# Projection and feed-forward output computed token-major, gates read as rows from a DRAM scratch

## What is computed

```
mod = cond @ ada_w.T + ada_b              # per sequence: six rows of 128
sh_msa, sc_msa, g_msa, sh_mlp, sc_mlp, g_mlp = split(mod, 6)
h  = modulate(rmsnorm(x), sh_msa, sc_msa)
q, k, v = split(h @ qkv_w.T)              # 16 heads of 8; rmsnorm and rope on q, k
o  = softmax(q k^T) v
x  = x + g_msa * (o @ proj_w.T + proj_b)  # x1 in the kernel
h2 = modulate(rmsnorm(x), sh_mlp, sc_mlp)
ff = (silu(h2 @ w1.T) * (h2 @ w3.T)) @ w2.T
x  = x + g_mlp * ff                       # x2 in the kernel
... second block: layer norm, q/k/v, linear attention, layer norm, silu, out_W, gate
```

## Time and profile before

| | |
|---|---|
| time, median of 3 runs | 212.8 us (212.53 to 213.04) |
| profiled execution, its own time | 211.97 us |
| its span, first to last instruction | 210.2 us |
| PE busy in the span | 183.4 us, 87% |
| DVE, POOL, ACT busy | 164.0, 135.9, 130.7 us |
| granted TensorE clock, mean | 0.987 of 2.4 GHz |

### The profile page before, as it was taken

The page is one execution under the profiler, slowest core; times in us unless marked ns, Lnnn a source line. Parts: engine busy times, 40 slices in busy tenths (PEclk is TensorE's granted clock), DMA queues, the critical chain, the costliest instruction groups (busy, mean ns, idle before and its releaser), DMA issues.

```text
span 210.2 us, 5867 instructions
## 1 busy us (share of the span) xinstructions
PE 183.4 (87%) x1986; PEld 141.1 (67%) x1986; DVE 164.0 (78%) x488; ACT 130.7 (62%) x354; POOL 135.9 (65%) x346
## 2 busy tenths in 40 slices
PE   1796868889999999899999999999998799998742
PEld 1544556667777777777776787788886478887522
DVE  4798898897979799996666434778899589999851
ACT  1476696677777777676555784453432367999740
POOL 8889798989786867758800783167512546757642
PEclk9999999999999999999999999999999999999995
DMA  5963000000000000000000000000000000001102
GB/s 111 280 178 142 0 5 3 0 0 3 3 3 2 3 6 0 3 3 2 3 3 0 3 3 0 2 0 0 6 0 0 0 2 3 0 25 30 51 26 74
DMA packets 9915, 5.13 MB, mean 24 GB/s; under 512 B 3025, under 2 KB 9758, under 8 KB 9758
## 3 DMA queue, kind: packets, MB, share of 16 engines
q1 hardware_dynamic: 6494, 4.08, 6.4%
q10 hardware_dynamic: 3392, 0.68, 1.6%
HBM read 3.71 MB, written 1.05 MB: 23 GB/s over the span
## 4 chain that ended last, share of the span: by engine, by line
PE 61%; DVE 21%; ACT 6%; issue 6%; POOL 2%; ACTq 2%; POOLq 0%; DVEq 0%
PE bank L1769 8%; DVE qkpad L1500 8%; PE bank L1778 7%; PE bank L1860 6%; PE bank L799 5%; PE bank L810 5%; PE bank L800 5%; PE bank L786 4%; PE bank L920 3%; PE bank L1801 2%; PE bank L1837 2%; PE bank L1872 2%; PE bank L852 2%; ACT probs L1201 2%; PE bank L1830 2%
## 5 line engine op out<-in xcount | busy, mean ns | idle before, releaser
L1201 ACT ACTIVATE probs<-bank 128x512 f32<-128x512 f32 x64 | 34.7, 594 | 22.6 <-PE bank L1778 22.5
L1500 DVE TENSOR_REDUCE qkpad<-bank 128x4 f32<-128x512 f32 x64 | 41.0, 684 | 9.1 <-PE bank L1769 7.7
L1778 PE MATMUL bank<-qTm,kBD 32*128 32x128 f32 x512 | 37.1, 283 | 0.4 <-ACT probs L1201 0.4
L1769 PE MATMUL bank<-kBD,qTs 32*128 32x256 f32 x224 | 31.7, 399 | 5.7 <-DVE qkpad L1500 4.2
L1778 PEld LDWEIGHTS bank<-qTm,kBD 32*128 32x128 f32 x512 | 31.0, 186 | 1.0 <-ACT probs L1201 0.6
L1769 PEld LDWEIGHTS bank<-kBD,qTs 32*128 32x128 f32 x224 | 19.8, 184 | 10.8 <-DVE qkpad L1500 7.4
L545 ACT ACTIVATE th<-bank 128x256 f32<-128x256 f32 x24 | 9.2, 384 | 18.9 <-PE bank L800 15.5
L1860 PE MATMUL bank<-probs,vpad 128*32 128x128 f32 x512 | 18.5, 277 | 0.2
L1051 POOL TENSOR_TENSOR partner<-qk,rope 128x96 f32<-128x96 f32 x32 | 14.3, 467 | 6.7 <-ACT qk L1243 6.7
L1801 PE MATMUL bank<-ident,qkpad 128*128 128x128 f32 x96 | 16.5, 281 | 0.8 <-DVE qkpad L1598 0.8
L481 POOL TENSOR_SCALAR var<-mv 128x2 f32<-128x2 f32 x16 | 3.1, 193 | 20.3 <-DVE mv L672 18.4
(11 more groups left out here) (250 smaller groups left out, 512.3 us busy)
## 6 DMA issues: line engine op xcount, KB each, us to landing
gate<-in_cond_dram SPq DMA_DIRECT2D x1, 1024.0 KB, 4.6
out_dram<-res SPq DMA_DIRECT2D x8, 128.0 KB, 1.8
xin<-in_x_dram ACTq DMA_DIRECT2D x2, 256.0 KB, 5.1
xin<-in_x_dram SPq DMA_DIRECT2D x1, 512.0 KB, 4.9
ada_n<-in_L_cond_ada_w_dram SPq DMA_DIRECT2D x1, 256.0 KB, 5.2
w_n<-in_L_cond_w_dram SPq DMA_DIRECT2D x2, 128.0 KB
qkv_n<-in_L_cond_qkv_w_dram SPq DMA_DIRECT2D x1, 192.0 KB, 3.9
w_n<-in_L_cond_w_dram SPq DMA_DIRECT2D x1, 170.5 KB
```

The source lines that it names most:

```text
L1201: q.activation(probs[2 * r + i][:, :, :, :].rearrange("p f a t -> p (f a t)"), bank[E_BANK[i]][:, :], ACT.Exp, scale=SCALE).then_inc(s_p, 1)
L1500: q.tensor_reduce(out_, score_bank(b, r, i)[:, :].rearrange("p (f a t) -> p f a t", f=2, a=2), X_AXIS, ALU.max, negate=True).then_inc(s_ma ...
L1769: last = q.matmul(bank[S_BANK[i]][:, f * 2 * T:(f + 1) * 2 * T], qTs[b % 2][rows, f, :], kBD[b % NKB][rows, f, :, :].rearrange("p a t -> p ...
L1778: last = q.matmul(bank[E_BANK[i]][:, (2 * f + k) * T:(2 * f + k + 1) * T], kBD[t % NKB][rows, f, k, :], qTm[t % 2][rows, f, :], start=True ...
```

## The change

The gates of the attention projection (`modr[:, 2]`), of its bias (`gbias`) and of the feed-forward (`modr[:, 5]`) are turned into rows on PE, copied by ACT, written to a DRAM scratch and read back by three DMAs that spread each over all partitions (`g1_rows`, `bias1_rows`, `g2_rows`, 1 MB each, in buffers that are free then: x2, y, res). POOL multiplies `projT` with the gate row of each sequence (`scaled_projection`) and adds the bias row to the input (`input_biased`). The projection has `oT` stationary and the scaled matrix moving, its result is token-major, and DVE adds the input straight from it. `projected` on ACT and `projected_turned` on PE are gone, batch statistics on DVE are replaced by a square with a sum on ACT, and `rms1` shrinks from seven operations to two. In the feed-forward `back` has ff stationary and w2T moving, two matmuls of 128 columns into banks 2 and 3 in place of one of 256; DVE multiplies both with the gate rows into `fg`, and POOL adds x1 (DVE for units 6 and 7). The transposes of fg are gone. `std2` of units 5 to 7 moves one place back on POOL's queue.

```
@@ blocks_gpsimd
+                cols = pair(u)
+                g.wait_ge(s_sq1, UNIT * u + UNIT)
+                q.tensor_scalar(ms1[:, cols], ms1[:, cols], 1.0, EPS0, ALU.mult, ALU.add).then_inc(b_ms, 1)
+                g.wait_ge(b_ms, u + 1)
                 q.tensor_tensor(rstd1[:, cols], ms1[:, cols], minus_half[:, 0:UNIT], ALU.pow).then_inc(b_rstd, 1)
...
+            def after_feed_forward(u):
...
+                g.wait_ge(b_fg, u + 1)
+                if u == 0:
+                    g.wait_ge(s_pg, B)
+                q.tensor_tensor(x2[:, pair(u), :], fg[u % 2][:, :, :], x1[:, pair(u), :], ALU.add).then_inc(b_x2, 1)
...
+            for u in range(start, U):
+                if u + 2 < U:
+                    rms1(u + 2)
+                normed1(u)
+                after_feed_forward(u - 3)
+                std2(u - 5)
+            after_feed_forward(U - 3)
+            std2(U - 5)
             std2(U - 4)
-            std2(U - 3)
...
+                if 1 <= t <= 3:
+                    std2(U - 4 + t)
@@ blocks_vector
-            def b_fed(t):
-                if is_unit(t):
-                    v.wait_ge(b_fm, t + 1)
...
+            def spread2(u):
+
+                v.wait_ge(b_x2, u + 1)
...
             def b_rest(t):
                 gated_(t, 0)
...
                 gated_(t, 1)
                 gate_(t, 2)
                 if is_unit(t):
-                    v.wait_ge(b_fgT, t + 1)
...
+                    v.wait_ge(b_fm, t + 1)
+                    if t == 0:
+                        v.wait_ge(ld_g2, 16)
+                    wait(v, b_x2, t - 1)
+                    for j in range(UNIT):
+                        last = q.tensor_tensor(fg[t % 2][:, j, :], bank[F_BANK[j]][:, 0:D], g2_rows[:, UNIT * t + j, :], ALU.mult)
+                    last.then_inc(b_fg, 1)
+                    if t >= JOINED:
...
+                        q.tensor_tensor(x2[:, pair(t), :], fg[t % 2][:, :, :], x1[:, pair(t), :], ALU.add).then_inc(b_x2, 1)
                 gated_(t, 2)
...
+                for u in ((t,) if t >= JOINED + 1 else (t - 1, t) if t == JOINED else (t - 1,)):
+                    if is_unit(u):
+                        spread2(u)
@@ blocks_tensor
-                    last = q.matmul(bank[F_BANK][:, 0:UNIT * T], w2T[:, c, :], ff[c][:, :], start=c == 0, stop=c == FC - 1)
+                    for j in range(UNIT):
+                        last = q.matmul(bank[F_BANK[j]][:, 0:D], ff[c][:, j * T:(j + 1) * T], w2T[:, c, :],
+                                        start=c == 0, stop=c == FC - 1)
...
-                if is_unit(t):
-                    e.wait_ge(b_fg, t + 1)
-                    wait(e, b_x2, t)
-                    turned(bank[FT_BANK], lambda j: fg[:, j, :], b_fgT)
@@ sync
+            sp.wait_ge(pv_a, A_ROWS)
+            sp.dma_start(scratch.rearrange("c b f -> b c f"), rows[:, :, :]).then_inc(ld_rows, 16)
+            sp.wait_ge(ld_rows, 16)
+            sp.dma_start(g1_rows[:, :, :], scratch[0, :, :].partition_broadcast(128)).then_inc(ld_g1, 16)
+            sp.dma_start(bias1_rows[:, :, :], scratch[1, :, :].partition_broadcast(128)).then_inc(ld_gb1, 16)
+            sp.wait_ge(pv_a, A_SQUARES)
+            sp.dma_start(g2_rows[:, :, :], scratch[2, :, :].partition_broadcast(128)).then_inc(ld_g2, 16)
@@ gpsimd
+            def scaled_projection(b):
...
+                g.wait_ge(ld_g1, 16)
+                g.wait_ge(pv_a, A_DONE)
+                wait(g, s_proj, b - 1)
+                q.tensor_tensor(projTg[b % 2][:, :], projT[:, :], g1_rows[:, b, :], ALU.mult).then_inc(s_pg, 1)
+
+            def input_biased(b):
...
+                g.wait_ge(ld_gb1, 16)
+                g.wait_ge(pv_a, A_SQUARES)
+                g.wait_ge(s_xs, b + 1)
+                q.tensor_tensor(xin[:, b, :], xin[:, b, :], bias1_rows[:, b, :], ALU.add).then_inc(s_xb, 1)
...
                 turned_own(t + 5)
-            blocks_gpsimd(g)
+                scaled_projection(t - 1)
+                input_biased(t - 1)
...
@@ scalar
-            def projected(b):
...
+            def spread_of(b):
...
+                a.wait_ge(s_x1, b + 1)
+                wait(a, s_sq1, b)
+                q.activation(squared[:, :], x1[:, b, :], ACT.Square, scale=D ** -0.5, accum_out=ms1[:, b:b + 1]).then_inc(s_sq1, 1)
...
+            q.activation(rows[:, :, :].rearrange("b c f -> b (c f)"), bank[O_BANK][0:B, 0:3 * D], ACT.Copy).then_inc(pv_a, 1)
             square_sums_of_rows()
@@ vector
-                v.wait_ge(s_prT, b + 1)
-                q.tensor_tensor(x1[:, b, :], bank[P_BANK][:, 256:384], xin[:, b, :], ALU.add).then_inc(s_x1, 1)
...
+                v.wait_ge(s_proj, b + 1)
+                v.wait_ge(s_xb, b + 1)
+                q.tensor_tensor(x1[:, b, :], bank[P_BANK][:, 384:512], xin[:, b, :], ALU.add).then_inc(s_x1, 1)
@@ tensor
                 e.wait_ge(s_oT, b + 1)
-                q.matmul(bank[P_BANK][:, 384:512], projT[:, :], oT[:, :], start=True, stop=True).then_inc(s_proj, 1)
+                e.wait_ge(s_pg, b + 1)
+                wait(e, s_x1, b)
+                q.matmul(bank[P_BANK][:, 384:512], oT[:, :], projTg[b % 2][:, :], start=True, stop=True).then_inc(s_proj, 1)
```

160 lines of the change are left out of this document (78 added, 82 removed).

## The result

| | before | after |
|---|---|---|
| time, median | 212.92 us (212.53 to 213.21, 4 runs) | 222.84 us (221.55 to 223.11, 4 runs) |
| profiled execution | 211.97 us | 222.69 us |
| its span | 210.2 us | 221.0 us |
| PE busy in the span | 183.4 us | 184.3 us |

The change makes the kernel slower by 4.6%: the ratio of the times is 1.0459, with a 95% interval from 1.0432 to 1.0485. The forecast was 220.9, with a range from 217.3 to 225.0. Of the 10.8 us that the span grew by, only 0.9 is busy time of PE (the net of matmuls that are gone and of stretches in which they run at half the clock), and 9.9 is PE waiting. An execution more than 1.5% above the fastest of its kernel is left out of the comparisons; there is one, in e7.

A forecast was written before the change was run, and what follows sets the result against it. PE bounds the feed-forward; a chain from DVE's row maxima through PE sets attention's 6.07 us step. Terms +2.7 - 0.3 + 0.3 + 6.3 - 0.9 = +8.1 on 211.97 give 220.1, plus 0.8 for the median 220.9; range 217.3 to 225.0.

The forecast's parts named there:

- step 3: Attention: PE's projection waits for POOL's scaled matrix, so round 1 starts at 52.95 instead of 50.86, +2.1 us.
- clock behind step 3: Attention, PE's clock after the long projection wait: no loss was forecast.
- steps 5 to 12: Attention: the loop through qk, Newton steps, POOL's product and projection becomes the bound at even POOL iterations, +0.6 us.
- steps 15 and 16: Where attention meets feed-forward: removing L1830 ahead of PE work without slack saves 0.2 and 0.1, together -0.3 us.
- `back` of unit 1: Feed-forward, first wait for the late fg: partly hidden, as PE waits for the last sequence's projection anyway, +0.3 us.
- `back` of units 2 to 6: Feed-forward: PE waits for DVE's fg, now behind yg2, five times, +6.3 us in all.
- `back` of unit 7: Feed-forward, last unit: first matmuls of the second block stand in between, so no loss, 0.
- start of the second block: Second block: PE's wait for xs3 of unit 2 goes and the last unit's fg and x2 get shorter, -0.9 us.
- the rest of the second block: Second block after its start: no change counted, 0.
- term of 1.27 a step: Feed-forward: 1.49 us of idle PE ahead of `back`, less 0.22 for removed transposes, +1.27 us a step.
- rival "faster": Whole kernel: fg doesn't hold up PE and POOL delivers in time, so only removals count, 209.4 us; chance 8%.
- The clock: Feed-forward rival: PE idle a quarter of each step falls to half clock, +20 us, giving 241; chance 3%.

The follow-up runs named there:

- e7: Kernel before, with only DVE's fg moved behind yg of part 2 and nothing else of the change; 224.17 us, ratio 1.0530.
- e1: Changed kernel, with DVE's products fg moved from behind yg2 to behind ff0; 212.43 us, ratio 0.9996 to the kernel before.
- e3: Changed kernel, with both fg earlier on DVE and the scaled matrix earlier on POOL; 210.60 us, ratio 0.9892 to the kernel before.
- e8: Changed kernel, without POOL's bias products and DVE's wait for them; 221.37 us, ratio 1.0409 to the kernel before.
- e2: Changed kernel, with the scaled matrix made earlier in POOL's iteration, ahead of the Newton steps; 219.49 us, ratio 1.0319 to the kernel before.
- e5: e3 with x2 of unit 5 on DVE and its statistics in the same step; 210.89 us, ratio 0.9921 to the kernel before.
- e9: e6 and e5 together, plus statistics of unit 7 behind knb of unit 0 on DVE; 210.76 us, ratio 0.9908 to the kernel before.
- e6: e3 with the bias of sequences 0 and 1 added by DVE instead of POOL; 210.28 us, ratio 0.9898 to the kernel before.

## Why the prediction held, and where it didn't

| term | forecast | measured |
|---|---|---|
| step 3 | +2.1 | +2.0 |
| clock behind step 3 | none | +1.2 |
| steps 5 to 12 | +0.6 | +0.4 |
| steps 15 and 16 | -0.3 | -0.4 |
| `back` of unit 1 | +0.3 | +0.5 |
| `back` of units 2 to 6 | +6.3 | +7.3 |
| `back` of unit 7 | 0 | -0.15 |
| start of the second block | -0.9 | -0.75 |
| the rest of the second block | 0 | +0.75 |
| sum | +8.1 | +10.8 |

The column "measured" takes the differences of the two profiled executions at the places of the first table.

**The feed-forward** was right in its mechanism: e1 takes it away and e7 puts it into the other kernel. The term of 1.27 a step was too small by 0.2. From PE's last `hidden` matmul to `back` the forecast reckoned 1.49 and the trace has 150.13 - (148.12 + 0.43) = 1.58, because PE started 0.14 after the end of DVE's fg (the piece "issue" in the chain), where the forecast had taken the 0.03 that DVE needs after a tanh. Another 0.1 is `back` itself: up to the next start its parts occupy 0.52 and 0.89 us, and 0.44 and 0.86 before. In e1, without the wait, it is 0.45 and 0.89, so of that only 0.04 belongs to the smaller matmuls. The rival "faster" (209.4) comes near what is left without the two placements: e3 measures 210.6, with a wait of 0.89 in step 3 still in it.

**Step 3** came out well, since POOL's queue was counted instruction by instruction; its product takes 0.45 against the 0.44 interpolated from the earlier trace rows. The 0.1 of the table flatters it: +2.1 is the forecast for round 1 and +2.0 is measured at the projection. Like with like, the projection was forecast for 51.70 and starts at 51.40, and round 1 for 52.95 and starts at 52.69. Both are 0.3 early because POOL, in this execution, ends L1086 ahead of its first product at 42.47 + 0.72 = 43.19, not at 43.49. Steps 5 to 12 kept to the pattern of small losses at the even iterations. That the way round the loop bounds them was right (e8). That POOL's load at the same time bounds step 3 stood in the prediction only as "POOL has no idle time ahead of that", and its consequence, that an earlier product would merely move part of the wait, showed in e2.

**The clock** is the term that the prediction lacks. It asked whether the feed-forward would lose it and gave 3% to a loss of 20 us. It stayed up there, through five idle times of 1.42, and fell in attention behind the one of 1.89, which the prediction itself had forecast and did not follow any further. That is 1.2 us of the 2.7 that the sum is short; another 1.1 is the feed-forward, and 0.75 the end, with 0.3 back from small terms.

**The second block** gained its 0.75 of 0.9, by another way than told. xs3 of unit 2 no longer waits, but xs3 of unit 1 does, for 0.99, behind `std2` of unit 5, whose statistics now come one step later. The prediction had the new place of `std2` and overlooked the new place of the statistics that it reads. It named what would be late next, the kx chain, and e5 and e9 show that. The gain then went at the end. The last 9 us before (with the clock at 0.70) and after (0.54):

```profile
201.20:210.20 9.00, 2.91 (x15) 1.95 (x14) 2.45 (x7) 1.23 (x3) 3.24 (x5) 0.70 0.17 50
```

```profile
212.00:221.00 9.00, 3.75 (x14) 2.50 (x14) 2.45 (x7) 1.22 (x3) 2.57 (x4) 0.54 0.14 44
```

The same work of the last units takes 0.84 us more of PE at the lower clock. Since executions differ in this, it is a property of the profiled one as much as of the kernel.

The median moved by 9.9, less than the 10.7 between the two profiled executions. That the forecast of 220.9 is only 1.9 off is in part luck, since two misses have opposite signs: the sum was 2.7 short against the profiled execution, and the profiled execution of before lay 0.9 below its median while that of after lay 0.15 below its own.

## What to carry to other kernels

When a step is moved on an in-order engine, look first at who overwrites its input. fg did not take longer, it only stood behind a result of the very matmul after which PE had nothing else to do, and that cost some 8 of the 10.8 us. Price such a wait from release to start on the next engine (0.14 us here, plus the slower first matmuls), not by the idle column, which showed 1.42 where 1.66 was lost. And where a sum contains one long idle time of PE, give the stretch behind it at the lower clock as a second case, with its price. Before a wait in one trace is held against the same wait in another, look whether both engines come to it equally early: a PE that is late for another reason hides it (e6).
